# The two adjacent value sums of an attention group are set apart in TensorE's order

## What is computed

```python
q = (x @ Wq).reshape(b, n, 32, 16)            # 4 sequences, 512 queries, 32 heads of 16
k, v = jnp.split(ctx @ Wkv, 2, axis=-1)       # 512 keys per sequence
q = apply_axial_rope(q, pos_map)
k = apply_axial_rope(k, ctx_pos_map)
logits = jnp.einsum('bqhd,bkhd->bhqk', q, k) * scale
w = jax.nn.softmax(logits, axis=-1)
attn = jnp.einsum('bhqk,bkhd->bqhd', w, v)
return attn.reshape(b, n, 512) @ Wout + bout
```

## Time and profile before

| | us |
|---|---|
| median of 3 runs | 1544.18 |
| lowest, highest | 1541.59, 1547.58 |
| time of the profiled execution | 1553.45 |
| span of its trace | 1551.6 |
| TensorE busy (modelled), of the span | 1433.4 |
| VectorE busy | 1107.3 |
| ScalarE busy | 998.5 |

### The profile page before, as it was taken

One profiled execution on the slowest core, in us unless ns is written; L12 is line 12 of the kernel. 1 busy time (PEld: TensorE's weight loads), 2 busy tenths in 40 slices (PEclk: granted clock), 3 DMA queues, 4 the chain that ended last, 5 costly groups with the idle time before them and its releaser, 6 DMA issues. The chain is left out here.

```text
span 1551.6 us, 20793 instructions
## 1 busy us (share of the span) xinstructions
PE 1433.4 (92%) x6045; PEld 616.3 (40%) x6057; DVE 1107.3 (71%) x1629; ACT 998.5 (64%) x1544; POOL 656.3 (42%) x438
## 2 busy tenths in 40 slices
PE   5798988988988989999999899699999999999999
PEld 2344434434444434444444344133333333244444
DVE  7999999999995522222222488899999989547985
ACT  3999998998974102323332254487887888868764
POOL 0689799699976431056566565200000000310000
PEclk7799999989998999999999999699999999999999
DMA  5212314113206337979953666323223223430464
GB/s 189 67 54 83 96 55 114 49 56 109 75 0 213 118 127 149 197 195 264 294 181 98 195 202 164 101 76 96 76 74 92 80 74 89 154 109 14 88 144 121
DMA packets 181210, 183.45 MB, mean 118 GB/s; under 512 B 104611, under 2 KB 132643, under 8 KB 180371
## 3 DMA queue, kind: packets, MB, share of 16 engines
q1 hardware_dynamic: 114422, 128.02, 28.6%
q10 hardware_dynamic: 57776, 24.89, 7.1%
q0 software_dynamic: 8944, 29.70, 6.4%
HBM read 96.97 MB, written 54.92 MB: 98 GB/s over the span
## 5 line engine op out<-in xcount | busy, mean ns | idle before, releaser
L1933 DVE TENSOR_REDUCE a_mx<-a_s 128x2 f32<-128x1024 f32 x256 | 303.4, 1219 | 34.0 <-PE a_s L2050 31.1
L284 POOL TENSOR_TENSOR m_hs<-m_hs,m_C 128x1024 f32<-128x1024 f32 x128 | 301.6, 2378 | 55.2 <-DVE m_hs L509 54.4
L509 DVE TENSOR_TENSOR_SCAN m_hs<-m_dA,m_d 128x512 f32<-128x512 f32 x256 | 294.5, 1200 | 12.7 <-PE m_d L664 11.4
L664 PEld LDWEIGHTS m_d<-ident_sb,m_dBuT 128*128 128x128 f32 x1024 | 119.9, 148 | 140.3 <-DVE m_hs L509 69.5
L664 PE MATMUL m_d<-ident_sb,m_dBuT 128*128 128x128 f32 x1024 | 162.1, 294 | 14.3 <-DVE m_hs L509 7.3
L390 ACT ACTIVATE m_dA<-m_dt,m_negA 128x512 f32<-128x512 f32 x256 | 167.8, 710 | 11.6 <-DMA m_dt<-m_dt 11.0
L1381 PE MATMUL e_gu<-e_w,e_xgT 128*128 x376 | 169.2, 593 | 0.1
L1772 POOL TENSOR_TENSOR x_sb<-x_sb,bo_sb 128x512 f32<-128x512 f32 x16 | 19.7, 1288 | 336.8 <-DVE a_m L1949 336.8
L368 ACT ACTIVATE m_dBuT<-m_dtuT,m_BT 128x512 f32<-128x512 f32 x241 | 157.8, 711 | 0.1
L2050 PE MATMUL a_s<-ring_sb 96*128 96x512 bf16 x512 | 152.3, 390 | 5.9 <-DVE a_mx L1933 4.1
L679 PE MATMUL m_y<-m_hs,m_fold 128*64 128x512 f32 x512 | 144.5, 645 | 3.6 <-POOL m_hs L284 3.6
(11 more groups left out here) (349 smaller groups left out, 2381.8 us busy)
## 6 DMA issues: line engine op xcount, KB each, us to landing
e_w<-in_ex_gu SPq DMA_DIRECT2D x16, 1024.0 KB, 8.5
ring_sb<-qk_dram SPq DMA_DIRECT2D x64, 192.0 KB, 3.0
xg_dram<-zeros_sb SPq DMA_DIRECT2D x47, 256.0 KB, 3.0
yg_dram<-attn_sb ACTq DMA_DIRECT2D x47, 256.0 KB, 4.0
m_C<-c_dram SPq DMA_DIRECT2D x64, 128.0 KB, 2.9
m_dt<-m_dt SPq DMA_DIRECT2D x64, 128.0 KB, 2.4
e_w<-in_ex_dn SPq DMA_DIRECT2D x16, 512.0 KB, 9.5
ring_sb<-qk_dram SPq DMA_DIRECT2D x64, 128.0 KB, 3.2
```

What stands on the lines that cost most here:

```text
L284: pool.tensor_tensor(hs[:, J % RH], hs[:, J % RH], C2[:, N % RC].unsqueeze(1).broadcast_to([P, 2, L]), ALU.mult).then_inc(s_hc, 1)
L509: dve.tensor_tensor_scan(hs[:, J % RH, h], dA[:, j % RA], pd[j % RD][:], 0.0, ALU.mult, ALU.add)\
L664: last = pe.transpose(pd[j % RD][:, t * P:(t + 1) * P], dBuT[:, N % 2, t, g], ident[:])
L1933: dve.tensor_reduce(mx[:, r % 2, h * TB + 2 * c:h * TB + 2 * c + 2], psc[c][:], AX.X, ALU.max)\
```

## The change

The second `v` of the list moves from beside the first one to behind `m0 k1`. Nothing else is changed: the same instructions, waits and buffers, in another place of one engine's queue. ScalarE, VectorE, GpSimd and the transfers have nothing at a `v`, so their order is the same.

```diff
     RG = 4
-    STEP = "q k0 k1 k2 v v k2 q m0 k1 q k2 k0 k1 q k2 v k1 q k0 q k1 k2 v c q k0 k1 k2 n q".split()
+    STEP = "q k0 k1 k2 v k2 q m0 k1 v q k2 k0 k1 q k2 v k1 q k0 q k1 k2 v c q k0 k1 k2 n q".split()
     KEYS = [int(s[1]) for s in STEP if s[0] == "k"]
```

## The result

The changed kernel took 1554.31 us (median of 5 runs, 1549.81 to 1557.11), the kernel before 1544.18 (5 runs): a ratio of 1.0053, 95% interval 1.0027 to 1.0079. It is slower, since the interval leaves out 1: by 8.2 us by the ratio and 10.1 by the medians; the prediction said 11.6, and 1555.8 for the median. A second comparison of the two kernels gave 1.0057, 1.0033 to 1.0081.

The account below looks back on a forecast made before the run. TensorE was taken to set the pace of steps 1 to 29, with VectorE close behind. Per step +0.23 + 0.30 - 0.13 = +0.40 us, over 29 steps +11.6: 1544.18 + 11.6 = 1555.8 us, range 1549 to 1562.

Parts of the forecast that it names:

- Entry and exit: TensorE, each full step: one more value-sum block to enter (0.09) and leave (0.14), +0.23 us.
- Rival B: The block has no price to enter and leave: +0.17 us per step, 4.9 us, 1549.1; no separate chance given.
- The stall: Second product into bank 2, each full step: TensorE waits for ScalarE's exponential, +0.30 us, up to 0.44.
- Rival A: Exponential in time, so no stall: +0.10 us per step, 2.9 us, 1547.1; chance 0.07.
- The wait of 0.13 that goes: Fourth pair by query, each full step: TensorE's wait for VectorE's maxima disappears, -0.13 us.
- VectorE's chain from the seventh pair: From a step's seventh pair to the next step's second maximum; said to decide the pair that waited 0.13.
- TensorE's reaction: Delay from the end of an awaited instruction to TensorE's start: 0.05 to 0.19 us, 0.05 taken.
- Rival D: Slower still: reaction 0.19 (15.7 us, 1559.9), or a further wait behind the moved block (17.4, 1561.6); chance 0.12.
- rival C: VectorE sets the pace, TensorE's hidden slack absorbs 0.53, only -0.13 counts: -3.8 us, 1540.4; chance 0.05.
- Steps 30 and 31: Last steps, without pairs by query: +0.25 in step 30, about as much regained in 31; 0 together, 0.5 either way.

Follow-up runs that it names:

- e2: Kernel before, with its double value sum taken apart by the first product into bank 2 alone: 11.91 us a step, ratio 1.0031.
- e5: Changed kernel, with the bank of the second and third product by key exchanged: 11.81 us a step, ratio 1.0001 to the kernel before.
- e1: Changed kernel, with a pair by query between first value sum and second product into bank 2: 11.83 us a step, ratio 1.0017 to the kernel before.
- e3: Kernel before, with the second product into bank 2 directly behind the first and both value sums behind it: 13.15 us a step, ratio 1.0309.
- e6: Kernel before, with the second value sum moved past one product only, the second into bank 2: 12.25 us a step, ratio 1.0107.
- e4: Kernel before, with the last two value sums side by side as well: 12.19 us a step, ratio 1.0102.

## Why the prediction held

**Entry and exit, +0.23.** Right. The moved block shows 0.31 and 0.99 in the trace of the changed kernel, though its neighbours are others than those of the rows that the price was read from. Around bank 2, where nothing else changes, it costs 0.23 in step 10 and 0.21 on average (e2). Rival B, that the block has no price, falls. The price isn't that of a change from bfloat16 to float32 as such. The turn of the summed values is float32 too, but takes the whole array, and in the trace of the kernel before it has no such price:

```profile
1104.28 0.38 PE L2076 MATMUL a_pv<-ring_sb 99*128 99x512 bf16 x1
1104.49 0.60 PE L2100 MATMUL a_pv<-ident_sb,a_aT 128*128 128x128 f32 x4
1104.93 1.03 PE L2050 MATMUL a_s<-ring_sb 96*128 96x512 bf16 x4
```

It is entered after 0.21 (1104.28 to 1104.49), and its four products take 0.44 until the pair by query behind them, 0.11 each. So the price goes with the value sums, whose products stand side by side in the array. What it consists of isn't shown. At the exit, the load of the next weights starts only together with its product, both at 1108.38.

**The stall, +0.30.** Right: 0.31 in the rows and 0.31 by e5. Rival A falls. The reason is shown from three sides: the stall goes when a pair by query covers it (e1), goes when ScalarE reaches that exponential earlier (e5), and grows to 1.39 when nothing stands between the products (e3).

**The wait of 0.13 that goes.** The size was right and the reason wrong. I put it down to VectorE's chain from the seventh pair. It hangs on the second pair: pair, 0.63 to its maximum, 1.22 to 1.23 for it and 0.05 to react are 1.90 to 1.92, against 1.79 of products. In the changed kernel it goes because the moved block stands between the second pair and the fourth. It stays where that distance is as before (e2, e6). By both reasons the wait goes in the changed kernel, so it is in part luck that this term came out right; e6 tells them apart, with 12.25 where my reason gave 12.35 and the other 12.2.

**TensorE's reaction.** The choice of 0.05 was right, and the upper bound of 0.19 was an error of reading. Rival D's first half falls with it. Its second half, a further wait later in the step, isn't seen either: the step is 0.42 longer on average, and the parts read in step 10 are 0.23, 0.31 and -0.13, together 0.41.

**The pace of VectorE (rival C).** TensorE had no hidden slack for the delay to fall into, since the step grew by the whole 0.42. VectorE doesn't set the pace in either kernel; with a second double block (e4) TensorE waits for it. Its idle time grew by (43.2 - 31.6) / 29 = 0.40 per step, as forecast.

**Steps 30 and 31.** The attention grew by 378.04 - 366.14 = 11.90 us, the 29 steps by 351.35 - 339.30 = 12.05. The end gave back 0.15, within the 0.5 that was allowed. Step 30 lost 0.10 and not 0.25 (its first value sum to that of step 31 is 10.62 us, 1338.20 to 1348.82, and was 10.52, 1340.44 to 1350.96): the turn followed the split by 0.05 and not by the 0.19 that I had put in. Step 31 and what follows it gave back 0.25, as forecast.

**The total.** 11.6 was forecast for the attention and 11.90 came. The ratio says 8.2, with an interval of 4.2 to 12.2 us. Of the difference, 1.2 to 1.7 us lie behind the attention, which the prediction had as unchanged. This leaves 10.2 to 10.7, inside the interval of the ratio. The other 2 us or so aren't attributed; the parts ahead of the attention differ by 10 to 13 us between traces of one kernel, enough to hide them.

## What to carry to other kernels

When one engine sets the pace of a hand-ordered loop, count the changes of kind in its queue as well as its instructions, and for each buffer that is reused the distance between its two uses against the chain that frees it. Here 1.73 us of products stood against 2.03 of exponentials, and one exchange of two banks took the stall away. A block that keeps the engine away from a second, nearly full one belongs where that engine has other work.

Read a wait from its own instruction and not from a merged row divided evenly; a row can hide a hole of a tenth of a microsecond. Where a kernel scatters by 10 us in parts that weren't touched, compare the stage between two fixed instructions: it repeated to 0.02 us here.

## What the runs showed of the hardware

At a granted clock of 1.00, a column-tiled float32 block between bfloat16 products cost 0.09 us to enter, from a product by key into bank 1 or bank 2, and 0.14 to leave, to a product by key or a pair by query. A float32 block on the whole array cost neither. In the rows shown, TensorE began a waiting weight load or product 0.05 to 0.06 us after the end of the instruction it waited for, for ScalarE and VectorE alike. Maxima that stood ready in VectorE's queue started 1.13 us apart, though each took 1.22. The granted clock behind the attention differed between kernels whose code there is the same, in one pair of traces behind the same idle time of 2.28 us, and the part took 1.2 to 1.7 us longer where the clock had fallen.
